# Graph attention with a routed feed-forward on one core: q in two float32r parts in the slots of the running sums, and the first loads of the edge loop moved ahead

## What is computed

```python
h = layernorm(x)
q, k, v = h @ Wq + bq, h @ Wk + bk, h @ Wv + bv            # each (n, H, C)
e = (edge_attr @ We).reshape(-1, H, C)
kj = k[src] + e
alpha = einsum('ehc,ehc->eh', q[dst], kj) / sqrt(C)
ea = exp(alpha - segment_max(alpha, dst)[dst])
alpha = ea / (segment_sum(ea, dst)[dst] + 1e-16)
out = segment_sum((v[src] + e) * alpha[:, :, None], dst).reshape(n, H * C) + (h @ Ws + bs)
x = x + out
x = x + routed_feed_forward(layernorm(x))                   # 8 experts, the best 2 of each node
```

## Time and profile before

| what | us |
|---|---|
| median of 3 runs (2594.77 to 2598.54) | 2597.56 |
| the profiled execution | 2597.09 |
| its span, first to last instruction | 2595.3 |
| busy: TensorE / VectorE / GpSimd / ScalarE | 2426.1 / 2003.4 / 1876.6 / 1595.2 |

### The profile page before, as it was taken

The page is one execution under the profiler, slowest core; times in us unless marked ns, Lnnn a source line. Parts: engine busy times, 40 slices in busy tenths (PEclk is TensorE's granted clock), DMA queues, the critical chain, the costliest instruction groups (busy, mean ns, idle before and its releaser), DMA issues. The chain is left out here.

```text
span 2595.3 us, 69745 instructions
## 1 busy us (share of the span) xinstructions
PE 2426.1 (93%) x14190; PEld 1972.0 (76%) x14191; DVE 2003.4 (77%) x5204; ACT 1595.2 (61%) x4422; POOL 1876.6 (72%) x2234
## 2 busy tenths in 40 slices
PE   5997999999999999999999999999996556999998
PEld 2444788888888888888888888878884546999998
DVE  5874899999999999999999999998996873222222
ACT  1232577667677677766777777766774124666665
POOL 5444688888888888888888888888885203666666
PEclk9998999999999999999999999999998557999999
DMA  7334888778788777777778778777872762433443
GB/s 221 127 109 145 237 226 227 219 223 226 220 225 226 221 224 225 224 222 224 225 226 226 227 222 225 227 221 216 226 223 72 214 185 56 71 64 63 69 67 54
DMA packets 337703, 476.84 MB, mean 184 GB/s; under 512 B 61318, under 2 KB 268492, under 8 KB 337052
## 3 DMA queue, kind: packets, MB, share of 16 engines
q0 software_dynamic: 92576, 259.72, 39.2%
q1 hardware_dynamic: 238492, 213.23, 26.8%
q10 hardware_dynamic: 6288, 0.05, 0.1%
HBM read 425.40 MB, written 50.57 MB: 183 GB/s over the span
## 5 line engine op out<-in xcount | busy, mean ns | idle before, releaser
L830 POOL DMA_INDIRECT kv_ring<-vk_table,tab_c x880 | 867.5, 986 | 281.2 <-issue 213.3
L985 PE MATMUL ps_e<-we_sb,aT 128*128 128x256 f32 x3520 | 912.7, 382 | 8.7 <-DVE ve_ke L1075 6.3
L1069 DVE TENSOR_TENSOR ve_ke<-kv_ring,ps_e 128x512 f32<-128x512 f32 x880 | 601.9, 684 | 93.7 <-PE ps_e L989 31.8
L985 PEld LDWEIGHTS ps_e<-we_sb,aT 128*128 128x128 f32 x3520 | 601.4, 191 | 62.2 <-ACT aT L918 7.4
L840 POOL TENSOR_TENSOR w_ring<-ve_ke,ea 128x264 f32<-128x264 f32 x880 | 569.1, 650 | 22.6 <-PE ps_u L1037 6.2
L1037 PE MATMUL ps_u<-w_ring,sel 128*128 128x264 f32 x1760 | 543.9, 391 | 8.8 <-DVE acc L1135 4.5
L918 ACT COPY aT<-ps_t 128x256 f32<-128x256 f32 x880 | 326.5, 371 | 334.3 <-PE ps_t L973 190.0
L989 PE MATMUL ps_e<-q_parts,selT 128*128 x2640 | 432.7, 273 | 0.0
L1135 DVE TENSOR_TENSOR acc<-acc,ps_u 128x264 f32 x880 | 369.9, 420 | 25.6 <-issue 9.3
L1056 DVE TENSOR_REDUCE alpha<-ve_ke 128x8 f32<-128x256 f32 x880 | 366.2, 416 | 6.3 <-issue 4.1
L1075 DVE TENSOR_TENSOR ve_ke<-ve_ke,ps_e 128x256 f32<-128x256 f32 x880 | 361.6, 411 | 1.9
(11 more groups left out here) (247 smaller groups left out, 2699.7 us busy)
## 6 DMA issues: line engine op xcount, KB each, us to landing
a_ring<-in_edge_attr SPq DMA_DIRECT2D x880, 128.0 KB
loc_c<-loc_table SPq DMA_DIRECT2D x220, 128.0 KB
kv_ring<-vk_table,tab_c POOLq DMA_INDIRECT x880
vk_table<-kv_out SPq DMA_DIRECT2D x49, 256.0 KB
skip_table<-skip_out SPq DMA_DIRECT2D x49, 128.0 KB
q_parts<-skip_table SPq DMA_DIRECT2D x7, 896.0 KB, 10.4
xn_table<-acc SPq DMA_DIRECT2D x7, 896.0 KB, 6.6
out<-q_parts SPq DMA_DIRECT2D x1, 6144.0 KB
```

What stands on the lines that cost most here:

```text
L830: g.indirect_dma_start(out=kv_ring[:, i % N_KV, :], out_offset=None, in_=vk_table, in_offset=bass.IndirectOffsetOnAxis(ap=tab_c[:, c % N_T ...
L985: t.matmul(ps_e[i % 2][:, 0:D], aT[i % 2][:, k * P:(k + 1) * P], we_sb[:, k, :], start=(k == 0), stop=(k == KD - 1))
L1069: v.tensor_tensor(both, kv.rearrange("p (t h c) -> p t h c", t=2, c=C), by_head(e, C)[:, None, :, :].to_broadcast([P, 2, H, C]), ALU.add). ...
```

## The change

- q is kept in two float32r parts: ScalarE's rounded copy, and GpSimd's difference to it. Both lie in one array of slots, 520 words to a node tile, one slot further on than the running sums and x1 of that tile will lie. The selection is float32r too.
- The running sums are no longer cleared: the first item of a tile multiplies the previous slot by 0, later ones their own by 1 (same_tile).
- A slot holds 256 sums and then 8 counts, in place of 8 heads at pitch 33. exp is written beside the values, GpSimd weighs the 256 values in place, and its ring is gone with the wait for the sum four items ago. The rescale is one instruction for the sums, one for the counts.
- We, the first four edge tiles, and the first chunk's tables and three rows of loc are loaded by SyncE ahead of the stores of node tile 43, into memory that now belongs to both blocks.
- What shared memory with q or the sums later on has memory of its own.

```diff
+        with ExitStack() as first_use:
+            q_slots = sb("q_slots", [P, NT + 2, SLOT], F32R, first_use)
+        node_slots = sb("node_slots", [P, NT + 2, SLOT])
+        q_first, q_second = [q_slots[:, 1:NT + 2, k * D:(k + 1) * D] for k in range(2)]
+        q_moving = [q_slots[:, :, :].rearrange("p j w -> p (j w)")[:, SLOT + k * D:] for k in range(2)]
+        x_sb = node_slots[:, 1:NT + 1, D:2 * D]
...
+                def edge_loop_inputs():
+                    sp.dma_start(we_sb[:, :, :], We.rearrange("(k p) n -> p k n", p=P)).then_inc(we_loaded, 16)
+                    for i in range(N_A):
+                        row = sp.value_load(item_row[0:1, i:i + 1], min_val=0, max_val=E - P)
+                        sp.dma_start(a_ring[:, i, :], edge_attr[bass.ds(row, P), :]).then_inc(a_loaded[i], 16)
+                    sp.wait_ge(tables_written, 16 * (1 + 3 * (2 if n_last else 1)))
+                    sp.dma_start(tab_c[:, 0, :, :].rearrange("p t i -> p (t i)"), tab_table[:, 0:3 * CH]).then_inc(tab_loaded[0], 16)
+                    sp.dma_start(run_c[0][:, :], run_table[0:CH, :][:, None, :].to_broadcast([CH, H, P])).then_inc(run_loaded[0], 16)
+                    sp.dma_start(resets[0][:, 0:P], reset_table[0:CH, :][:, None, :].to_broadcast([CH, H, P])).then_inc(reset_loaded[0], 16)
+                    for n in range(NLOC - 1):
+                        sp.dma_start(loc_c[n][:, :], loc_table[n:n + 1, :].to_broadcast([P, SEL * P])).then_inc(loc_loaded[n], 16)
+
                 for j in range(NT):
                     par = j % 2
+                    if j == NT - 6:
+                        edge_loop_inputs()
...
-                def third_part(j):
-                    pool.wait_ge(s["q_part1"], at("q_part1", j))
-                    g.tensor_tensor(q_parts[:, 2, j, :], q_left[j % 2][:, :], q_parts[:, 1, j, :], ALU.subtract
-                                    ).then_inc(s["q_part2"], 1)
...
-                def clear(k):
-                    pool.wait_ge(s["skip_out_ready"], at("skip_out_ready", last_x_under(k)))
-                    g.memset(acc[:, k, :], 0.0).then_inc(s["acc_cleared"], 1)
...
+                def second_part(j):
+                    pool.wait_ge(s["q_first_ready"], at("q_first_ready", j))
+                    pool.wait_ge(s["skip_out_ready"], at("skip_out_ready", j))
+                    g.tensor_tensor(q_second[:, j, :], q_full[j % 2][:, :], q_first[:, j, :].bitcast(F32), ALU.subtract
+                                    ).then_inc(s["q_second_ready"], 1)
...
+                v.memset(same_tile[:, 0:1], 0.0)
+                then(v.tensor_tensor(same_tile[:, 1:IT], node_tile_rep[:, 1:IT], node_tile_rep[:, 0:IT - 1], ALU.is_equal))
...
+            selT = [sb3(f"selT{i}", [P, SEL * P], F32R) for i in range(2)]
...
-                    pool.wait_ge(s["summed"], at("summed", m - N_W))
-                    g.tensor_tensor(by_head(w_ring[:, i % N_W, :], CP), by_head(ve_ke[:, par * CH + i, :], CP),
-                                    ea[par][:, i * H:(i + 1) * H][:, :, None].to_broadcast([P, H, CP]),
+                    ve = by_head(ve_ke[:, par * CH + i, 0:D], C)
+                    g.tensor_tensor(ve, ve, ve_ke[:, par * CH + i, D:UW][:, :, None].to_broadcast([P, H, C]),
                                     ALU.mult).then_inc(s["weighted"], 1)
...
-                            nc.scalar.activation(ea[1 - par][:, :], ps_x, ACT.Exp, scale=-SCALE)
+                            nc.scalar.activation(ve_ke[:, (1 - par) * CH:(2 - par) * CH, D:UW], by_head(ps_x, H), ACT.Exp, scale=-SCALE)
...
-                    for part in range(3):
+                    for part in range(2):
                         last = t.matmul(ps_e[i % 2][:, D:2 * D], selT[i // SEL % 2][:, i % SEL * P:(i % SEL + 1) * P],
-                                        q_parts[:, part, :, :].rearrange("p j d -> p (j d)")[:, bass.ds(n * D, D)],
-                                        start=(part == 0), stop=(part == 2))
+                                        q_moving[part][:, bass.ds(n * SLOT, D)], start=(part == 0), stop=(part == 1))
...
-                    v.tensor_tensor(a, a, factor[:, :, None].to_broadcast([P, H, CP]), ALU.mult).then_inc(s["rescaled"], 1)
+                    v.tensor_tensor(a, a, factor[:, :, None].to_broadcast([P, H, C]), ALU.mult).then_inc(s["values_rescaled"], 1)
+                    v.tensor_tensor(held, held, factor[:, :], ALU.mult).then_inc(s["rescaled"], 1)
+                    dve.wait_ge(s["values_rescaled"], at("values_rescaled", c))
                     dve.wait_ge(s["rescaled"], at("rescaled", c))
...
-                    v.tensor_tensor(a, a, ps_u[i % 2][:, 0:UW], ALU.add).then_inc(s["acc_added"], 1)
+                    v.scalar_tensor_tensor(out=to, in0=sofar, scalar=same_tile[:, m:m + 1], in1=ps_u[i % 2][:, 0:UW], op0=ALU.mult, op1=ALU.add
+                                           ).then_inc(s["acc_added"], 1)
```

More of the change, by code:

```diff
@@ L9 @@
 BF16 = mybir.dt.bfloat16
+F32R = mybir.dt.float32r
 ALU = mybir.AluOpType
@@ L195, in gnn_ffn @@
             q_full = [sb1(f"q_full{i}", [P, D]) for i in range(2)]
-            q_left = [sb1(f"q_left{i}", [P, D]) for i in range(2)]
             ps_t = [ps1(f"ps_t{i}", [P, 512]) for i in range(2)]
@@ L556, in masks @@
                         then(v.tensor_tensor(here[:, :], first_run[:, :], node_run[:, :], ALU.is_equal))
+                        then(v.tensor_tensor(here[:, :], here[:, :], same_tile[:, 0:IT:CH], ALU.mult))
                         then(v.scalar_tensor_tensor(out=carried[:, 1:NCH], in0=here[:, 1:NCH], scalar=SCALE, in1=runs_on[:, 1:NCH],
@@ L1334, in _ @@
                 assert NT % SG == 0
-                then(v.tensor_scalar(den[:, :], heads[:, :, C:CP].rearrange("p n c -> p (n c)"), 1e-16, None, ALU.add))
+                then(v.tensor_scalar(den[:, :, :], counts, 1e-16, None, ALU.add))
                 dve.sem_inc(den_step, 1)
-                v.reciprocal(inv[:, :], den[:, :]).then_inc(den_step, 1)
+                v.reciprocal(inv[:, :, :], den[:, :, :]).then_inc(den_step, 1)
                 dve.wait_ge(loaded, 16 * 3)
@@ L1397, in gnn_ffn @@
             nb = sb5("nb", [P, NBK])
-            rest = flat(acc[:, :, :])[:, TOP * NT * P:(NT + 1) * UW]
-            held, taker, unused, parts = [rest[:, i * NB:(i + 1) * NB] for i in range(4)]
-            in_lo = flat(acc[:, :, :])[:, 0:TOP * NT * P // 2].bitcast(BF16).rearrange("p (c f) -> p c f", f=P)
+            held, taker, unused, parts = [sb5(n, [P, NB]) for n in ("held", "taker", "unused", "parts")]
+            in_lo = [values[:, :, k * P // 2:(k + 1) * P // 2].bitcast(BF16) for k in range(TOP)]
             in_hi = sb("in_hi", [P, 2, NQ, NBK], BF16, c5)
```

197 lines of the change are left out of this document (78 added, 119 removed).

## The result

The changed kernel takes 2574.06 us (median of four runs, 2570.37 to 2577.29) against 2598.05 for the kernel before in the same comparison: ratio 0.991, 95% interval 0.9886 to 0.9927. It is faster by 0.9%, 24 us where the forecast said 68. The profiled run, the fastest of the four, took 2570.37 us with a span of 2568.6, so 26.7 us less than the profiled run of before. From the same instructions of both traces the 26.7 split as follows (forecast in brackets): the projections up to the last kv_out 2.1 us less (1 more), from there to the first score 11.2 less (11 less), first to last score **9.2 less (57 less)**, behind the last score 4.1 less (0). All that is missing is missing in the loop.

The account below looks back on a forecast made before the run. TensorE was taken to bound the edge loop, with the bound moving to VectorE. From 2597.1 us, less 57 for the loop and 11 for the switch, plus 1 for the prologue: 2530 us, range 2486 to 2582.

Parts of the forecast that it names:

- The q products: TensorE, edge loop: two float32r products at 0.11 us each replace three; tile 1.86 to 1.75 us, chunk to 29.67.
- The sign set for them: TensorE, edge loop: q records 0.11 us start to start; over 0.165 would prove the forecast wrong.
- The add: VectorE, edge loop: scalar_tensor_tensor costs a fixed 0.07 us more a tile, 1.1 us a chunk.
- The rescale: VectorE, once a chunk: a second instruction on 8 columns adds 0.1 us to 0.64, between 0 and 0.2.
- VectorE's new floor: Edge loop: VectorE needs 30.1 to 30.7 us a chunk, taken as 30.4, above TensorE's 29.67.
- The step that failed: Edge loop: chunk equals VectorE's floor, 30.4 us; TensorE's stalls lie inside it and GpSimd's weigh change counts 0.
- The term of 57 us: Edge loop: chunk falls 1.03 us, from 31.43 to 30.4, over 55 chunks.
- GpSimd or the three together bound: Edge loop rival: engines within 0.8 us a chunk couple; chunk 31.0 to 31.2, 2570 to 2580 us; chance 0.15.
- a sign of being wrong: Edge loop: a chunk outside 29.7 to 31.2 us would make the prediction wrong.
- The loads: Switch into the loop: first score 11 us earlier, bounds 7 to 12; late stores cost projections 0, at worst 3.
- The prologue and the stages behind the loop: Program start: one more VectorE tensor_tensor costs 1 us, 0 to 1.1; behind the loop 0, ±2.

Follow-up runs that it names:

- one_half: Changed kernel with one of its two q products left out and half of the value columns unweighed on GpSimd: 2539.0 us.
- plain_add: Changed kernel with the accumulation as a plain tensor_tensor add, the factor 0 or 1 left out, relieving VectorE: 2548.4 us.
- one_q: Changed kernel with only the first of its two float32r q products, relieving TensorE: 2565.6 us.
- before_two: Kernel before with two of its three bf16 q products, the third part left out: 2552.8 us.
- plain_one_half: Changed kernel with plain add (factor left out), one q product and half of the value columns unweighed: 2537.7 us.
- best: Changed kernel, nothing left out: rescale ahead of score, its wait ahead of add, second owner reduction behind add, three score banks, loads spread over tiles 37 to 47: 2538.1 us.

## Why the prediction was off

**The q products** held: 0.12 us each by the tile (forecast 0.11), tile 1.77 (forecast 1.75). The sign set for them, records under 0.165 us apart, does not apply, as their starts lie otherwise (above). The Trainium skill ("FP8 and Floating Point Precision", TensorE Precision Notes) gives four passes to true float32 and says of a reduced-precision form that it reads the 4-byte word and truncates it; a cost near that of bfloat16 fits this.

**The add** held: 0.06 us a tile (0.07), on 264 columns as on 128, so the scalar's cost is fixed and not by the column. **The rescale** was sized too low: 0.98 us in the chunk shown, where 0.74 was taken from 0.64 and 0.1. Its second instruction is followed by 0.31 us of waiting for itself, and its first is stretched beside GpSimd (562 against 424 ns).

**VectorE's new floor** was taken as 30.4 us a chunk, between 30.1 and 30.7; one_half, where VectorE is alone, has 30.12, the low end. The figure was 0.28 too high, and by luck this hid as much of the failed step.

**The step that failed** is the one after it: that the chunk would take what VectorE's floor says, with TensorE's stalls "inside VectorE's sum, not beside it" and GpSimd at "0 either way". The chunk took 30.77, 0.65 above one_half's 30.12. Relieving GpSimd alone brings 0.37 us of that, TensorE alone 0.10, both together all of it; none of these prices stood in the sum. Of GpSimd's part 0.14 us is seen in VectorE's rescale (562 to 424 ns), and TensorE's sum waits for the weigh now and then (5.6 us in 24 times from 400 to 1940 us); how the rest comes through is not shown. From the forecast's 30.4 to 30.77, at 55 chunks, it is 20 us of the missing 48.

**The term of 57 us was mis-sized besides.** It set a mean, 31.43 us a chunk, against a floor. The undisturbed chunk of before was 31.08; the difference are longer chunks that TensorE's saving could not shorten, and the changed kernel has them too: 0.35 × 55 = 19 us. Floor against floor the term would have been 31.08 − 30.4, 37 us, of which 17 came (31.08 − 30.77). The longer chunks became a little worse, 0.10 us each or 5 us; the last 3 lie at the ends of the loop.

**The rival** "GpSimd or the three together bound", with 2570 to 2580 us, is what happened; it had a chance of 0.15. The chunk's mean, 31.24 us, also lies just outside the 29.7 to 31.2 that the forecast set as a sign of being wrong. What spoke for it stood in the forecast, a GpSimd floor of 30.3 beside a VectorE floor of 30.4. Two floors 0.1 us apart are a reason to expect more than the larger one.

**The loads** held at the switch (11.2 for 11). In the projections they cost 2.2 us where I took 0 and allowed 3, and about 4 in the kernels whose clock falls there: the stores of tile 43 came 6 us late, the upper end, and VectorE waited for them.

**The prologue and the stages behind the loop** came out 3 to 5 us better than forecast: the idle time before the second kv_out shrank from 6.22 to 1.39 us, and the stretch behind the last score by 4.1. Why was not tried.

## What to carry to other kernels

When the floors of several engines lie within a few per cent, the time is not the largest of them: expect half or less of what an edit takes off one engine (0.40 of 0.96 us with plain_add, 0.10 of 1.76 with one_q), and some of what it adds to an engine that is not the bound. Set floors against floors, so take the undisturbed period of the loop and not its mean as what a saving starts from. An engine's wait for its own last instruction can be worth as much as its work: put an independent instruction there, and look in the trace whether the wait has gone or only moved, and what the moved instruction was hiding. Before a wait is put down to the input that is left over, look when each of its semaphores came.

## What the hardware showed

float32r products of 256 columns run nearly at the pace of bf16 ones: TensorE's tile is 1.77 us with two of them here and 1.75 with two bf16 ones in before_two, whose timeline is:

```profile
1004.21 1.03 PE L985 MATMUL ps_e<-we_sb,aT 128*128 128x256 f32 x4
1005.08 0.38 PE L989 MATMUL ps_e<-q_parts,selT 128*128 x2
1005.96 1.03 PE L985 MATMUL ps_e<-we_sb,aT 128*128 128x256 f32 x4
```

GpSimd stops ahead of the 114th gather and of every 110th behind it, at the same gathers in before, after, plain_one_half and best, for 1.7 to 3.9 us. Of the eight chunks over 31.7 us in the kernel after, six hold such a stop or follow it at once. The timeline of GpSimd in the kernel after, at one such place, and the table of stretches behind it:

```profile
1723.81 0.97 POOL L809 DMA_INDIRECT kv_ring<-vk_table,tab_c  x1 [0.36 <-issue]
1727.93 0.97 POOL L809 DMA_INDIRECT kv_ring<-vk_table,tab_c  x1 [3.15 <-DVE ve_ke L1044]
```

```profile
1727.00:1730.00 3.00, 0.40 (x3) 0.19 (x2) 1.63 (x5) 0.85 (x3) 2.05 (x4) 0.98 0.43 109
1730.00:1733.50 3.50, 3.50 (x11) 2.83 (x12) 0.73 (x2) 1.59 (x4) 3.15 (x5) 0.53 0.46 146
1733.50:1740.00 6.50, 6.50 (x40) 5.71 (x40) 6.04 (x17) 3.83 (x12) 4.85 (x7) 1.00 0.68 197
```

The gather needs the score of four tiles before it, which had ended by 1724.5. In all 28 of these stops the gather starts 3.45 to 3.47 us behind the end of that score; for the other gathers that VectorE is named for, the median is 0.79. So the 2.7 us beyond that are not VectorE's; what they are stays open. TensorE, busy 0.40 of 3 us in the first of these stretches, has a granted clock of 0.53 in the next 3.5 us (most of it the lower of its two levels, 1.2 instead of 2.4 GHz) and 1.00 behind it. The chunk is 4.6 us longer than an undisturbed one (35.35 and 30.77), with a stop of 3.15 us in it.
